# Eight batches in place of four in the rings of the edge layers, the scatter and the last stage of a graph network

## The reference, cut to what matters

```python
# layer 1, edge MLP (the layer in front of it is an attention layer with gathers of its own)
msg_input = jnp.concatenate([x[src], x[dst], edge_attr], axis=-1)
h = jax.nn.relu(msg_input @ W1.T + b1)
agg = jax.ops.segment_sum(h @ W2.T + b2, dst, num_segments=x.shape[0])
# layer 2, filter layer
W = ssp(edge_attr @ mlp_w0.T + mlp_b0) @ mlp_w2.T + mlp_b2
agg = jax.ops.segment_sum(c[:, None] * (W * h1[src]), dst, num_segments=h.shape[0])
# layer 3, gated layer: means over both directions
a_in = _seg_mean(feat_in[src], dst, N)
a_out = _seg_mean(feat_out[dst], src, N)
```

## Time and profile before

| | us |
|---|---|
| median of 3 runs | 8541.56 (8523.47 to 8550.98) |
| the profiled execution | 8520.73, its span 8519.0 |
| POOL busy | 4943.0 (58% of the span) |
| PE / PEld busy | 4534.8 (53%) / 3543.4 (42%) |
| DVE busy | 3925.8 (46%) |
| ACT busy | 1191.4 (14%) |

### The profile page before, as it was taken

How to read it: one execution, slowest core, us unless ns; L and a number is a source line. 1 busy time by engine, 2 the same in 40 slices (tenths; PEclk the granted TensorE clock), 3 DMA queues, 4 the chain that set the end, 5 groups by cost and what they waited for, 6 DMA issues and landing times. The chain is left out here.

```text
span 8519.0 us, 96589 instructions
## 1 busy us (share of the span) xinstructions
PE 4534.8 (53%) x23978; PEld 3543.4 (42%) x23978; DVE 3925.8 (46%) x10258; ACT 1191.4 (14%) x2445; POOL 4943.0 (58%) x5229
## 2 busy tenths in 40 slices
PE   4222322267525666664577777633333237878776
PEld 3121222156424444443455555522222137777764
DVE  7444444589863343335555545530000025555555
ACT  2000000000030010111434444421111100000003
POOL 1677776244336666665566666536666666666652
PEclk7555555566767777766677777755555556666668
DMA  2555555333304444443222222322222223333340
GB/s 77 138 152 152 151 153 152 59 99 97 91 22 116 117 117 117 117 116 53 59 59 59 60 59 60 42 58 66 65 66 66 64 59 91 90 91 89 90 74 16
DMA packets 608391, 741.26 MB, mean 87 GB/s; under 512 B 124392, under 2 KB 435569, under 8 KB 607869
## 3 DMA queue, kind: packets, MB, share of 16 engines
q1 hardware_dynamic: 452094, 389.34, 17.2%
q0 software_dynamic: 155776, 345.75, 16.5%
HBM read 539.56 MB, written 198.34 MB: 87 GB/s over the span
## 5 line engine op out<-in xcount | busy, mean ns | idle before, releaser
L678 POOL DMA_INDIRECT e_ring<-table,gather_i x1760 | 1808.7, 1028 | 974.5 <-issue 503.2
L678 POOL DMA_INDIRECT at_ring<-keys_values,gather_i x880 | 939.3, 1067 | 444.0 <-issue 253.7
L709 DVE TENSOR_TENSOR arena<-arena,e_pa 128x128 f32 x1760 | 497.9, 283 | 1480.5 <-remote 645.2
L1557 POOL DMA_INDIRECT rows_by_src<-rs_out,key x880 | 856.3, 973 | 539.1 <-ACT rs_out L1542 274.7
L678 POOL DMA_INDIRECT bw_ring_f<-table,gather_i x880 | 847.2, 963 | 458.0 <-issue 235.6
L1532 PE MATMUL rs_ph<-arena,rs_hot_t 128*128 x2640 | 419.6, 284 | 959.6 <-ACT rs_out L1542 535.4
L1249 PE MATMUL e_pa<-e_msg,e_hot 128*128 128x128 f32 x3520 | 679.9, 347 | 466.0 <-DVE e_msg L1293 313.7
L777 PE MATMUL at_pq<-arena,at_hot_t 128*128 x2640 | 392.8, 291 | 994.3 <-DVE at_hot_t L788 581.8
L1249 PEld LDWEIGHTS e_pa<-e_msg,e_hot 128*128 128x128 f32 x3520 | 602.7, 254 | 547.4 <-DVE e_msg L1293 329.3
L777 PEld LDWEIGHTS at_pq<-arena,at_hot_t 128*128 128x128 bf16 x2640 | 274.5, 104 | 1112.9 <-issue 1054.9
L1532 PEld LDWEIGHTS rs_ph<-arena,rs_hot_t 128*128 128x128 bf16 x2640 | 274.5, 104 | 1104.7 <-issue 1039.4
(11 more groups left out here) (403 smaller groups left out, 8387.8 us busy)
## 6 DMA issues: line engine op xcount, KB each, us to landing
rows_by_src<-e_filler SPq DMA_DIRECT2D x220, 260.0 KB
bw_ring_r<-rows_by_src SPq DMA_DIRECT2D x220, 260.0 KB
edge_values<-at_ring SPq DMA_DIRECT2D x220, 256.0 KB
as_ring<-edge_values SPq DMA_DIRECT2D x220, 256.0 KB, 2.6
at_rows<-local_rows SPq DMA_DIRECT2D x220, 128.0 KB
e_rows<-local_rows SPq DMA_DIRECT2D x220, 128.0 KB
e_ring<-table,gather_i POOLq DMA_INDIRECT x1760
rs_rows<-local_rows SPq DMA_DIRECT2D x220, 128.0 KB
```

What stands on the lines that cost most here:

```text
L678: pool.indirect_dma_start(ring[:, r, u, :], None, table, bass.IndirectOffsetOnAxis(index, 0)).then_inc(arrived[r], 16)
L709: self.dve.tensor_tensor(to, to, self.psum[:, u, 0:self.width], ALU.add).then_inc(self.added, 1)
L1557: pool.indirect_dma_start(table, bass.IndirectOffsetOnAxis(place, 0), out[:, r, u, :], None, bounds_check=SLOTS - 1, oob_is_err=False).the ...
```

## The change

`DEEP` = 8 is the new depth of these rings: the gathered rows of `stage_edges` in both layers and of the forward direction of `stage_both_ways`, the packed rows `rs_out` of the scatter, the rows `bw_ring_r`, and the broadcast rows of local indices (`e_rows` in layer 1, `rs_rows`). Each slot has a semaphore of its own, so eight take the place of four. The gathered rings, `rs_out` and the rows of layer 1 move into free parts of the arena. The attention scores keep four. The one-hots, the attributes and the PSUM buffers keep their depths in all stages. No engine gets another instruction or another order; only the waits count from eight batches back.

```diff
+DEEP = 8
-def gather_rows(pool, c, table, ring, arrived, freed):
+def gather_rows(pool, c, table, ring, depth, arrived, freed):
     for k in range(BATCHES):
-        i, r = k // R, k % R
+        i, r = k // depth, k % depth
...
-                at_least(pool, sem, per * (k - R + 1), None)
+                at_least(pool, sem, per * (k - depth + 1), None)
@@ stage_edges
-        ring = sb("ring", [P, R, U, F])
+        ring = arena(c, room, [DEEP, U, F])
...
-            hot_t, rows = sb("hot_t", [P, R, U, P], BF16), sb("rows", [P, R, U * P], BF16)
+            hot_t, rows = sb("hot_t", [P, R, U, P], BF16), arena(c, room + DEEP * U * F, [DEEP, U * P], BF16)
...
-            gather_rows(pool, c, table, ring, arrived, [(freed, 1)])
+            gather_rows(pool, c, table, ring, DEEP, arrived, [(freed, 1)])
...
                 at_least(sp, ready, k - R + 1, tick)
                 if layer == 1:
-                    at_least(sp, hots_t, k - R + 1, tick)
-                    load_local_rows(sp, c, rows, k, r, rows_in)
+                    at_least(sp, hots_t, k - DEEP + 1, tick)
+                    load_local_rows(sp, c, rows, k, k % DEEP, rows_in)
...
-                    at_least(dve, arrived[r], 16 * U * (i + 1), tick)
+                    at_least(dve, arrived[k % DEEP], 16 * U * (k // DEEP + 1), tick)
                     at_least(dve, sent, k - 1, tick)
-                    dve.tensor_tensor(tmp[:, q, :, :], ph[:, q, :, :], ring[:, r, :, :], ALU.add).then_inc(first, 1)
+                    dve.tensor_tensor(tmp[:, q, :, :], ph[:, q, :, :], ring[:, k % DEEP, :, :], ALU.add).then_inc(first, 1)
@@ stage_rows_by_src
-        out = sb("out", [P, R, U, REV])
-        rows, hot_t = sb("rows", [P, R, U * P], BF16), sb("hot_t", [P, R, U, P], BF16)
+        out = arena(c, ACC0 + NT * F, [DEEP, U, REV])
+        rows, hot_t = sb("rows", [P, DEEP, U * P], BF16), sb("hot_t", [P, R, U, P], BF16)
...
-                at_least(sp, hots_t, k - R + 1, tick)
+                at_least(sp, hots_t, k - DEEP + 1, tick)
...
-                at_least(act, scattered[r], 16 * U * i, tick)
-                act.activation(out[:, r, :, F + 1], c.src_local[:, at], ACT.Copy).then_inc(packed, 1)
+                at_least(act, scattered[k % DEEP], 16 * U * (k // DEEP), tick)
+                act.activation(out[:, k % DEEP, :, F + 1], c.src_local[:, at], ACT.Copy).then_inc(packed, 1)
                 at_least(act, ready, k + 1, tick)
-                act.activation(out[:, r, :, 0:F], ph[:, r % 2, :, :], ACT.Copy).then_inc(packed, 1)
+                act.activation(out[:, k % DEEP, :, 0:F], ph[:, r % 2, :, :], ACT.Copy).then_inc(packed, 1)
@@ stage_both_ways
-        ring, hot = [sb("ring_f", [P, R, U, F]), sb("ring_r", [P, R, U, REV])], [sb("hot_f", [P, R, U, P]), sb("hot_r", [P, R, U, P])]
+        ring, hot = [arena(c, B2_0, [DEEP, U, F]), sb("ring_r", [P, DEEP, U, REV])], [sb("hot_f", [P, R, U, P]), sb("hot_r", [P, R, U, P])]
...
-            gather_rows(pool, c, c.table, ring[0], arrived[0], [(summed[0], 1)])
+            gather_rows(pool, c, c.table, ring[0], DEEP, arrived[0], [(summed[0], 1)])
...
-                at_least(sp, summed[1], k - R + 1, tick)
+                at_least(sp, summed[1], k - DEEP + 1, tick)
@@ the calls
-        stage_edges(nc, c, "e1_", c.table, acc, c.bucket_d, c.local_d, layer=1)
+        stage_edges(nc, c, "e1_", c.table, acc, c.bucket_d, c.local_d, layer=1, room=B1_0 + 3 * NT * F // 2)
-        stage_edges(nc, c, "e2_", c.table, acc, c.bucket_d, c.local_d, layer=2)
+        stage_edges(nc, c, "e2_", c.table, acc, c.bucket_d, c.local_d, layer=2, room=B2_0)
```

More of the change, by code:

```diff
@@ L748, in _ @@
         def _(pool):
-            gather_rows(pool, c, c.kv, ring, arrived, [(producted, 1), (kept, 16)])
+            gather_rows(pool, c, c.kv, ring, R, arrived, [(producted, 1), (kept, 16)])
         @block.sync
@@ L1123, in _, with stage_edges @@
             dve.wait_ge(added, BATCHES * U)
-def stage_edges(nc, c, name, table, acc, buckets, local, layer):
+def stage_edges(nc, c, name, table, acc, buckets, local, layer, room):
     with ExitStack() as ctx:
@@ L1135, in stage_edges @@
         pb = lambda n, s: ctx.enter_context(nc.psum_tensor(name + n, s, F32))
-        ring = sb("ring", [P, R, U, F])
+        ring = arena(c, room, [DEEP, U, F])
         hot = sb("hot", [P, R, U, P])
         pa = pb("pa", [P, 2, U, F])
-        arrived, attributes = [sem(f"arrived{r}") for r in range(R)], [sem(f"attributes{r}") for r in range(R)]
-        rows_in = [sem(f"rows{r}") for r in range(R)]
+        arrived, attributes = [sem(f"arrived{r}") for r in range(DEEP)], [sem(f"attributes{r}") for r in range(R)]
+        rows_in = [sem(f"rows{r}") for r in range(DEEP)]
         hots, summed, added, start, tick = (sem(n) for n in ("hots", "summed", "added", "start", "tick"))
@@ L1497, in stage_rows_by_src @@
         sb = lambda n, s, d=F32: ctx.enter_context(nc.sbuf_tensor("rs_" + n, s, d))
[L1498 to L1499 removed]
+        out = arena(c, ACC0 + NT * F, [DEEP, U, REV])
+        rows, hot_t = sb("rows", [P, DEEP, U * P], BF16), sb("hot_t", [P, R, U, P], BF16)
         ph = ctx.enter_context(nc.psum_tensor("rs_ph", [P, 2, U, F], F32))
[L1501 removed]
+        rows_in, scattered = [sem(f"rows{r}") for r in range(DEEP)], [sem(f"scattered{r}") for r in range(DEEP)]
         start, hots_t, ready, packed, tick = (sem(n) for n in ("start", "hots_t", "ready", "packed", "tick"))
@@ L1558, in _ @@
                                             bounds_check=SLOTS - 1, oob_is_err=False).then_inc(scattered[r], 16)
-            for r in range(R):
-                pool.wait_ge(scattered[r], 16 * U * BATCHES // R)
+            for k in range(BATCHES - DEEP, BATCHES):
+                pool.wait_ge(scattered[k % DEEP], 16 * U * (k // DEEP + 1))
 def stage_both_ways(nc, c, fwd, rev):
@@ L1599, in step @@
                         if way:
-                            ins = pe.matmul(to[:, 0:F + 1], lhs, ring[1][:, r, u, 0:F + 1], start=True, stop=True)
+                            ins = pe.matmul(to[:, 0:F + 1], lhs, ring[1][:, k % DEEP, u, 0:F + 1], start=True, stop=True)
                         else:
-                            pe.matmul(to[:, 0:F], lhs, ring[0][:, r, u, :], start=True, stop=True)
+                            pe.matmul(to[:, 0:F], lhs, ring[0][:, k % DEEP, u, :], start=True, stop=True)
                             ins = pe.matmul(to[:, F:F + 1], lhs, c.ones[:, 0:1], start=True, stop=True)
@@ L1617, in one_hot @@
                     if way:
-                        at_least(dve, arrived[1][r], 16 * (i + 1), tick)
-                    inside = ring[1][:, r, :, F + 1] if way else c.local_d[:, bass.ds(k * U, U)]
+                        at_least(dve, arrived[1][k % DEEP], 16 * (k // DEEP + 1), tick)
+                    inside = ring[1][:, k % DEEP, :, F + 1] if way else c.local_d[:, bass.ds(k * U, U)]
                     dve.tensor_tensor(hot[way][:, r, :, :], over(c.j[:, 0:P], U), wide(inside, P), ALU.is_equal).then_inc(hots[way], 1)
```

25 lines of the change are left out of this document (12 added, 13 removed).

## The result

| | before | after |
|---|---|---|
| median of 14 runs, us | 8545.0 (8523.5 to 8559.0) | 8565.7 (8554.0 to 8579.9) |
| after / before | | 1.0026 (95%: 1.0017 to 1.0034) |
| profiled execution, us (span) | 8520.7 (8519.0) | 8562.8 (8561.1) |
| first DMA of one stage to that of the next: edge MLP | 1567.1 | 1574.9 |
| filter layer | 1532.3 | 1551.2 |

The change makes the kernel about 21 us slower, where 47 us less were forecast. The time lies within the range given, but on the other side. The table's last four rows, read off POOL's first indirect DMA in each stage, say where: +7.8, +18.9, +2.1 and +11.0 us, with +2.2 ahead of them. The profiled execution of before lies 24 us under its median and that of after 3 us under its own, so the difference of the profiles, 42 us, is larger than that of the medians; which parts are real is for the experiments.

What follows compares the result with a forecast made beforehand. It took the users' pace to bound the gather stages, and POOL's waits amid other engines' silence the scatter. Profiled: 8520.7 - 59 (scatter) + 12 (starts and ends) = 8473.7 us; median: 8541.6 - 47 = 8494.6, rounded to 8494; range 8350 to 8570.

Steps and rivals of the forecast that it cites:

- The gather stages in the steady state: Edge MLP, filter layer, last stage: a deeper ring grants POOL no more credit, as users are slower; priced at 0.
- The scatter: Scatter stage: eight slots let ACT pack further ahead, giving POOL seven-batch trains and fewer waits; 59 us less.
- the fifth and sixth batch: Scatter: with free slots ACT packs two more batches at 2.1 us each before silence, at about 6011.7 and 6013.8.
- Rival (1): Scatter: silence counts, not the ring; ACT waits for PE's result and trains keep five batches; 8554 us, chance 0.22.
- Starts and ends: Three gather stages: longer first fill costs 0 to 20 us, ends return about 5; +4 each, +12 together.
- rival (4): Gather starts: users fall silent during the eight-slot fill, +60 us, and the scatter gains nothing; 8602 us, chance 0.13.
- (2): Scatter: runs without any pause because longer trains let a pack through now and then; 8357 us, chance 0.10.
- rival (3): Gather stages: POOL's waits go there too, 615 us, besides the scatter's 59; 7868 us, chance 0.10.
- a mechanism unknown: All engines but POOL: long unbroken indirect-DMA trains go with silence on PE, DVE and ACT, cause not given; no size.

Runs made afterwards that it cites:

- edges_deep: Eight slots only in the edge MLP and filter layer rings, four elsewhere, against the kernel before: 8529.8 against 8520.2 us, ratio 1.0008.
- edges_12: Twelve slots for gathered rows of the edge MLP and filter layer, four elsewhere, against the kernel before, on a chip without silences: ratio 0.9990.
- deep_nap_mid: The changed kernel's eight slots plus a 128x256 POOL memset behind each indirect-DMA batch, against the kernel before: 7781.2 against 7611.6 us, ratio 1.0232.
- nap_short: Kernel before (four slots) plus a 128x8 POOL memset behind each scatter batch, on a chip without silences: cost 1 us in the scatter.
- nap_long_again: Kernel before (four slots) plus a 128x1024 POOL memset behind each scatter batch, on a chip with silences: 8476.5 (one execution) against 8442.8 us.

## Why the prediction was wrong

**The gather stages in the steady state: right.** A ring that is always full grants one batch per use, from four slots or from eight. POOL's waits, its trains of three batches in the edge MLP (62 of them before, 59 after) and their number stayed. On a chip without silences the same argument holds for another reason, since POOL is late and no ring is ever full.

**The scatter: wrong, -59 forecast, 0 measured.** The step that failed is the one on the fifth and sixth batch, "at 2.1 us a batch it would pack the fifth at about 6011.7 and the sixth at about 6013.8, which is where silence sets in". I took ACT's stop at 6009.65 to be the ring's, for its copy waited 3.16 us for a slot, and put the silence behind it. The slot came at 6013.41 and the pack only at 6019.73, 6.11 us later: in that stretch ACT had its slot and lacked only PE's semaphore, whose update is recorded at 6019.70. PE's pace was right. The fifth batch's 12 matmuls ran at full pace in the window behind the one of the earlier trace rows and ended at 6011.81 (columns as in the earlier trace rows):

```profile
6010.00:6012.00 2.00, 1.78 (x12) 1.25 (x12) 0.08 (x1) 0.25 (x1) 1.70 (x2) 0.50 0.37 100
```

So for ACT the silence had set in two packs earlier than I put it, while PE still worked. Rival (1) has the wait, though it takes PE's late signal for a slow PE ("with a busier PE"). When two waits follow each other in one step, the second is what is left when the first is taken away: the 3.16 and 6.11 us of before have become one wait of 9.39. Rival (1) had 0.22 and deserved the most.

**Starts and ends: right in kind, too small, +12 forecast.** The bounds per stage were -5 and +20. The term that was mis-sized is the start: with 5 us back at the end, +4 net means 9 of the possible 20 us, and the second uses moved by 17 and 22, so users stood still through the added part of the first train. What I took for the end, some 5 us back, and for the middle, "if they go on at their pace, 0", made +4 of it. Measured: +7.8, +18.9 and +11.0 in the profiles of before and after, 38 us in all; the runs of parts give less (+11 for the filter layer and 0 for the edge MLP in edges_deep; +3, +6 and +8 us for the three on the third chip, against kernels with four slots there, 17 together), with 21 and 30 us between the medians. So the loss is shown, and how it splits over the stages is known to some 10 us only. What decides between 0 and 20 was in the profile: the other engines' silence during a long train, which I had described and then did not apply to the first train.

So rival (4) had the right mechanism for its first half and rival (1) for the scatter, as far as the silence and not the ring counts; the truth is their sum, 8541.6 + 0 + about 21. Rivals (2) and (3) fell: no pack more in mid-train, no wait of POOL less. The rule behind rival (3), from the Trainium skill ("Perfetto Trace Analysis", section "Optimization Strategy"), that a gap repeating on the engine that should be saturated can mean too few buffers, is only a "can", and here it is not so: POOL's repeated gap (2.4 us in the earlier trace rows, 3.4 to 3.6 us in the middle of all over 1.2) is there with four, eight and twelve slots on a chip with silences, and is gone with four and twelve on one without (with three slots two waits are left in the edge MLP).

**What I had as a mechanism unknown** is still unknown, but its place is clearer. It begins with PE's signals, which come late while PE's matmuls go on. It isn't in the kernel: the same program has it on three sets of runs and not on three others, with 10.8% between 8545 and 7620 us. Each set was one chip at one time, so a lasting property of the chip and a passing state of it are not told apart. The changed kernel without naps was not timed on a chip without silences; edges_12 and deep_nap_mid stand for it there, with no loss.

## What to carry to other kernels

A wait for a full ring disappears with a deeper ring only if the wait behind it, in the same step, is shorter: read the next wait of the waiting engine before you price the first, and look whether the work that it waits for is over by then. Where a ring's user is slower than its filler on average, depth buys nothing in the middle, and if a long fill disturbs the users it costs one fill at every stage's start. And before tuning around a stall, see whether it is there on another chip.

## What the runs showed of the hardware

- **The same program takes 7612 to 7621 or 8443 to 8545 us, by the set of runs, each on a chip of its own.** All of the difference lies in the stages with indirect DMAs: from its first indirect DMA to its last POOL takes 1329 and 1218 us in the attention scores, 1383 and 1129 in the edge MLP, 1365 and 1171 in the filter layer, 1318 and 1124 in the scatter, 1299 and 1144 in the last stage (the kernel before, and nap_short).
- **During an unbroken train of indirect DMAs, on some chips, PE's signals reach the others late, and PE's register operations slow down.** In the scatter of the kernel before, 82 of 220 packs of ACT came over 2 us after PE's last matmul, the slot and the copy (76 of them over 5 us), and none in nap_short; the signals from ACT to PE took at most 0.44 us. Of PE's register operations, 46 ns in the middle, 214 of 2640 took over 400 ns, up to 1.4 us, in the kernel before, and none over 60 ns in nap_short. DMA packets take about the same time on both kinds (a packet of 4160 bytes in the scatter 193 in the kernel before against 189 ns in edges_12, in the middle). The Trainium skill ("SBUF — State Buffer", section "SBUF: two separate sides") has DMAs and compute unable to slow each other; PE, which reads SBUF in the scatter's matmuls, does fall behind beside POOL's DMAs on some chips, whatever the path by which it happens.
- **A memset on POOL slows DVE's one-hot beside it.** The 211 in the scatter of nap_long_again were busy for 204.65 us, against 74.86 for 212 in the changed kernel, 0.97 against 0.35 us each. The memset takes 0.98. The columns are as above, DVE the third. The mean mixes two kinds: 89 of the 220 one-hots overlap a memset, took 1.13 to 1.93 us and ended 0.15 us after it, and the others took 0.35 to 0.63. The Trainium skill ("SBUF — State Buffer", section "Who interferes with whom") says that such a DVE operation and one of GpSimd can block each other fully and that the one issued first gets the ports. The full block agrees; the order doesn't, as far as records show it, for 88 of the 89 started before the memset that they outlasted. The rows:

```profile
5640.00:6920.00 1280.00, 375.91 (x2559) 267.12 (x2557) 204.65 (x211) 148.88 (x430) 1047.28 (x1079) 0.50 0.23 65
```

```profile
5690.00:6970.00 1280.00, 411.83 (x2544) 264.64 (x2544) 74.86 (x212) 142.52 (x424) 829.45 (x852) 0.50 0.22 64
```
